# Modulation rows evacuated by ScalarE, chunk 0 turned behind two of the six modulation products, and the first loads in another order

## The reference

```python
mod = (_silu(L0_c) @ L0_wmod).reshape(L0_c.shape[0], 6, 1, -1)
sa, ca, ga, sb, cb, gb = (mod[:, 0], mod[:, 1], mod[:, 2], mod[:, 3], mod[:, 4], mod[:, 5])
ga = (2 * (ga >= 0) - 1) * jnp.maximum(jnp.abs(ga), 0.25)
gb = (2 * (gb >= 0) - 1) * jnp.maximum(jnp.abs(gb), 0.25)
h = _layernorm(x, axis=-1) * (1 + ca) + sa
x = x + ga * _L0_attn_ref(h, ...)   # 3 layers: linear attention with exp features, 16 heads; MLP 256-1024-256
h = _layernorm(x, axis=-1) * (1 + cb) + sb
x = x + gb * _L0_ffn_ref(h, ...)    # 2 layers: windowed softmax attention, 8 heads; gated MLP
```

## Time and profile before

| | |
|---|---|
| median of 3 runs | 2784.8 us (2779.9 to 2787.41) |
| profiled execution, its own time | 2785.39 us |
| its span, first to last instruction | 2783.6 us |
| TensorE busy | 2638.3 us (95%) |
| TensorE weight loads busy | 2145.3 us (77%) |
| VectorE busy | 2231.8 us (80%) |
| ScalarE busy | 1516.9 us (54%) |
| GpSimd busy | 1459.1 us (52%) |
| mean granted TensorE clock | 0.987 |

### The profile page before, as it was taken

The page is one execution under the profiler, slowest core; times in us unless marked ns, Lnnn a source line. Parts: engine busy times, 40 slices in busy tenths (PEclk is TensorE's granted clock), DMA queues, the critical chain, the costliest instruction groups (busy, mean ns, idle before and its releaser), DMA issues.

```text
span 2783.6 us, 61439 instructions
## 1 busy us (share of the span) xinstructions
PE 2638.3 (95%) x21416; PEld 2145.3 (77%) x21416; DVE 2231.8 (80%) x5244; ACT 1516.9 (54%) x3106; POOL 1459.1 (52%) x1408
## 2 busy tenths in 40 slices
PE   6799999999999999999888999999999999999986
PEld 4577787878788877778676788888878787888875
DVE  7678877787677777887998888888888888888874
ACT  3454455444544454445336766667666566676651
POOL 2343444443443345344476766665566666767643
PEclk9999999999999999999999999999999999999998
DMA  3100000010000000000111100000011100001001
GB/s 100 28 9 9 17 2 16 9 38 2 1 1 16 11 26 20 16 24 17 57 35 44 32 17 12 15 16 14 29 32 29 29 25 23 30 29 32 29 19 36
DMA packets 77715, 65.63 MB, mean 24 GB/s; under 512 B 15378, under 2 KB 72682, under 8 KB 77418
## 3 DMA queue, kind: packets, MB, share of 16 engines
q1 hardware_dynamic: 77418, 61.70, 7.5%
HBM read 49.10 MB, written 12.58 MB: 22 GB/s over the span
## 4 chain that ended last, share of the span: by engine, by line
PE 57%; DVE 21%; ACT 10%; issue 8%; POOL 2%; DMA 0%; DVEq 0%; SPq 0%; POOLq 0%; ACTq 0%
PE PS L273 49%; DVE U L1497 4%; PE PS L758 3%; DVE X L1370 2%; DVE ZC L1568 2%; ACT U L1007 2%; ACT U L1006 2%; ACT U L1008 2%; DVE ST L1351 2%; ACT U L1009 1%; DVE Z L1362 1%; ACT FB L1033 1%; PE PS L711 1%; PE PS L720 1%; DVE Z L1450 1%
## 5 line engine op out<-in xcount | busy, mean ns | idle before, releaser
L1188 ACT ACTIVATE PR<-PS,SM 128x256 f32<-128x256 f32 (+1 forms) x512 | 279.4, 555 | 102.3 <-DVE SM L1689 100.8
L1033 ACT ACTIVATE FB<-PS,BC 128x512 f32<-128x512 f32 x192 | 132.4, 689 | 293.1 <-PE PS L273 290.6
L2029 POOL TENSOR_TENSOR RL<-FB,RH 128x512 fp32r<-128x512 f32 x96 | 124.2, 1294 | 276.9 <-DVE RH L1475 276.9
L1497 DVE TENSOR_TENSOR U<-PS,CST 128x512 f32<-128x512 f32 x384 | 236.5, 678 | 24.7 <-PE PS L273 24.7
L1684 DVE CUSTOM_DVE_ANT_0 PS<-PS,MSK 128x256 f32<-128x256 f32 (+1 forms) x512 | 202.8, 436 | 48.1 <-PE PS L273 46.8
L1041 ACT COPY NUM<-PS 128x256 f32<-128x256 f32 x96 | 35.9, 373 | 354.9 <-DVE TMP L1489 303.7
L273 PE MATMUL PS<-W2H,RH 128*128 128x256 f32 x768 | 222.7, 290 | 4.5 <-DVE RL L1478 3.9
L1475 DVE CAST RH<-FB 128x512 fp32r<-128x512 f32 x192 | 87.8, 457 | 171.0 <-ACT FB L1033 167.4
L2154 POOL TENSOR_TENSOR SM<-SM,COL 128x8 f32<-128x8 f32 x128 | 215.1, 1680 | 10.7
L273 PE MATMUL PS<-W2H,RL 128*128 128x256 f32 x768 | 215.8, 281 | 0.0
L273 PE MATMUL PS<-W2L,RH 128*128 128x256 f32 x768 | 215.3, 280 | 0.0
(11 more groups left out here) (233 smaller groups left out, 9003.7 us busy)
## 6 DMA issues: line engine op xcount, KB each, us to landing
PX<-in_L_attn_x SPq DMA_DIRECT2D x16, 512.0 KB, 4.0
TB<-in_k_rot SPq DMA_DIRECT2D x64, 128.0 KB, 2.1
SG<-in_L_attn_W SPq DMA_DIRECT2D x24, 256.0 KB, 2.7
xp_scratch<-PX SPq DMA_DIRECT2D x8, 512.0 KB, 3.1
xs_scratch<-X SPq DMA_DIRECT2D x64, 64.0 KB, 1.5
ZS<-xs_scratch SPq DMA_DIRECT2D x16, 256.0 KB, 2.9
GG<-xp_scratch SPq DMA_DIRECT2D x8, 512.0 KB, 3.8
out<-GG SPq DMA_DIRECT2D x8, 512.0 KB, 3.7
```

Source lines behind the costliest of these rows:

```text
L1033: e.activation(FB[:, hb % 2, :], PS[:, 5, :], ACT.Relu, bias=BC[:, l % 2, 4 + hb:5 + hb]).then_inc(*a_re.up(n, hb))
L1188: t = e.activation(PR[:, par, 256 * i + lo:256 * i + hi], PS[:, 3 + par, 256 * i + lo:256 * i + hi], ACT.Exp, bias=S[:, 40 + 2 * g + i:41 ...
L1497: e.tensor_tensor(heads(U[:, u % 6, :], 4), heads(PS[:, g, :], 4), bcast(CM, 4), ALU.mult).then_inc(*d_mk.up(n, u))
L2029: e.tensor_tensor(RL[:, r, :], FB[:, 0, :], RH[:, r, :].bitcast(F), ALU.subtract).then_inc(*p_rl.up(n, hb))
```

## The change

In the head all six products are evacuated by ScalarE, the rows that need "1 +" with an activation whose bias is 1. TensorE makes products 0 and 1, turns chunk 0, and makes products 2 to 5, the last two in banks 5 and 6. VectorE goes from the first weight split straight to chunk 0. The constants' semaphore is split in three (`s_col`, `s_cst`, `s_hs`), so that each reader waits for its own. The loads are issued in another order. The first two rounds are written out call by call; waits that stood in the loops moved into the helpers, and some are now repeated.

```diff
-    MODS = [(0, 0, 4), (1, 0, 5), (0, 1, 6), (1, 1, 7), (0, 2, 0), (1, 2, 1)]
+    MODS = [(0, 0, 4), (1, 0, 5), (0, 1, 6), (1, 1, 7), (0, 2, 5), (1, 2, 6)]
@@ TensorE
-            if n == 0 and i < 2:
-                e.wait_ge(*a_mod.at(5))
+            if n > 0:
+                e.wait_ge(*d_am.at(n - 1, 1))
...
+        def modulate(i):
+            b, j, bank = MODS[i]
+            e.wait_ge(*d_cb.at(3))
+            if i < 2:
+                e.wait_ge(*s_wm0.at(1))
+            else:
+                e.wait_ge(*s_wm.at(1))
+            if i >= 4:
+                e.wait_ge(*a_mod.at(i - 3))
             for k in range(2):
                 t = mm(e, PS[:, bank, :], FB[:, 0, 128 * (2 * b + k):128 * (2 * b + k) + 128], FQ[:, k, j, :], k == 0)
             t.then_inc(*e_mod.up(i))
...
+        modulate(0)
+        modulate(1)
         turn_x(0)
+        modulate(2)
+        modulate(3)
+        modulate(4)
+        modulate(5)
+        proj(0, 0)
@@ ScalarE
+            if i == 0:
+                e.wait_ge(*s_col.at())
+            if j == 0:
+                e.activation(MOD[:, b, D:2 * D], PS[:, bank, 256:512], ACT.Identity, bias=ONE)
+                t = e.copy(MOD[:, b, 0:D], PS[:, bank, 0:256])
...
+        copy_modulation(0)
+        copy_modulation(1)
+        copy_modulation(2)
+        high_row(0, 0)
+        high_row(0, 1)
+        copy_modulation(3)
+        copy_modulation(4)
+        copy_modulation(5)
@@ VectorE
         prologue(0)
         split(0)
-        split(1)
-        e.wait_ge(*e_mod.at(0))
-        e.tensor_copy(modulation(0, 0), PS[:, MODS[0][2], :]).then_inc(*d_mod.up(0))
-        e.wait_ge(*d_mod.at(0))
-        e.tensor_scalar(MOD[:, 0, D:2 * D], MOD[:, 0, D:2 * D], 1.0, None, ALU.add, ALU.bypass).then_inc(*d_mod.up(1))
-        e.wait_ge(*d_mod.at(1))
         modulate_a(0)
         modulate_b(0)
+        split(1)
...
-        e.tensor_scalar(MOD[:, 1, D:2 * D], MOD[:, 1, D:2 * D], 1.0, None, ALU.add, ALU.bypass).then_inc(*d_mod.up(2))
-        e.tensor_scalar(MOD[:, :, 4 * D:5 * D], MOD[:, :, 4 * D:5 * D], 1.0, None, ALU.add, ALU.bypass).then_inc(*d_mod.up(3))
...
+        state(0, 2)
+        masks(0, 3)
+        prologue(2)
+        modulate_a(2)
+        lower(1, 0, 2, 0, a_x, d_x)
+        lower(1, 1, 3, 0, a_x, d_x)
+        state(0, 3)
+        modulate_b(2)
@@ GpSimd
+        key_state(0, 1)
+        rsqrt(("p", 2))
+        key_state(0, 2)
+        key_state(0, 3)
@@ SyncE
-        load_x(0)
+        e.dma_start(COL[:, :], ins["k_col"]).then_inc(*s_col.up())
         wm = ins["L0_wmod"].rearrange("(k p) n -> p k n", p=128)
         for k in range(2):
             e.dma_start(FQ[:, k, 0, :], wm[:, k, 0:512]).then_inc(*s_wm0.up(k))
-        e.dma_start(CST[:, :, :], ins["k_cst"]).then_inc(*s_cst.up(0))
-        e.dma_start(COL[:, :], ins["k_col"]).then_inc(*s_cst.up(1))
+        load_x(0)
+        e.dma_start(CST[:, :, :], ins["k_cst"]).then_inc(*s_cst.up())
         load_piece(0)
         load_piece(1)
+        load_columns(0)
         for k in range(2):
             e.dma_start(FQ[:, k, 1:3, :], wm[:, k, 512:1536].rearrange("p (j n) -> p j n", j=2)).then_inc(*s_wm.up(k))
```

More of the change, by code:

```diff
@@ L460, in scores @@
         def scores(n, j):
+            if j == 0:
+                for i in range(2):
+                    e.wait_ge(*a_kt.at(n, i))
+                    if n > 0:
+                        e.wait_ge(*d_z.at(n - 1, i))
+                    else:
+                        e.wait_ge(*a_fe.at(n, i))
             for m in range(2):
@@ L549, in _ @@
             t.then_inc(*e_mod.up(i))
-            if i == 1:
-                e.wait_ge(*s_cst.at(4))
+        modulate(0)
+        modulate(1)
         turn_x(0)
-        for n in range(24):
+        modulate(2)
[3 more added lines that the diff above has]
+        proj(0, 0)
+        proj(0, 1)
+        proj(0, 2)
+        proj(0, 3)
+        values(0, 0)
+        values(0, 1)
+        favor(0, 0, 2)
+        favor(0, 1, 3)
+        favor(0, 2, 0)
+        favor(0, 3, 1)
+        turn_k(0, 0)
+        turn_k(0, 1)
+        key_sums(0)
+        scores(0, 0)
+        sums(0, 0)
+        scores(0, 1)
+        sums(0, 1)
+        scores(0, 2)
+        sums(0, 2)
+        scores(0, 3)
+        turn_x(1)
+        sums(0, 3)
+        spread(0)
+        proj(1, 0)
+        proj(1, 1)
+        proj(1, 2)
+        proj(1, 3)
+        values(1, 0)
+        values(1, 1)
+        favor(1, 0, 2)
+        favor(1, 1, 3)
+        favor(1, 2, 0)
+        favor(1, 3, 1)
+        attn_out(0, 0)
+        attn_out(0, 1)
+        turn_k(1, 0)
+        turn_k(1, 1)
+        key_sums(1)
+        scores(1, 0)
+        sums(1, 0)
+        scores(1, 1)
+        sums(1, 1)
+        scores(1, 2)
+        sums(1, 2)
+        scores(1, 3)
+        turn_h(0)
+        turn_x(2)
+        sums(1, 3)
+        for n in range(2, 24):
             live, w, m = n < 24, n - 1, n - 2
@@ L1054, in _ @@
             else:
-                e.copy(modulation(b, j), PS[:, bank, 0:256])
+                e.activation(MOD[:, b, 1024:1280], PS[:, bank, 0:256], ACT.Identity, bias=ONE)
                 t = e.copy(GB[:, b, :], PS[:, bank, 256:512])
             t.then_inc(*a_mod.up(i))
[L1058 to L1061, removed]
+        exponent()
+        copy_modulation(0)
+        copy_modulation(1)
+        copy_modulation(2)
@@ new lines, in _ @@
+        numerators(0, 3)
+        operands(1, 0)
+        operands(1, 1)
+        operands(1, 2)
+        operands(1, 3)
+        attention(0, 0)
+        attention(0, 1)
+        features(1, 0, 2)
+        features(1, 1, 3)
+        features(1, 2, 0)
+        features(1, 3, 1)
+        keep_rows(1, 0)
+        keep_rows(1, 1)
+        numerators(1, 0)
+        numerators(1, 1)
+        numerators(1, 2)
+        high_mid(0, 0)
+        high_mid(0, 1)
+        high_row(2, 0)
+        high_row(2, 1)
@@ L1525, in _ @@
         modulate_b(1)
[L1526 to L1529 removed]
+        add_bv(0, 0)
+        add_bv(0, 1)
+        split(3)
+        running(0, 0)
+        running(0, 1)
+        carry(0)
+        gate_steps(0)
+        gate_steps(1)
+        normaliser(0)
+        masks(0, 0)
+        split(4)
+        state(0, 0)
+        masks(0, 1)
+        split(5)
+        state(0, 1)
+        masks(0, 2)
+        split(6)
+        state(0, 2)
[6 more added lines that the diff above has]
+        modulate_b(2)
+        scale_num(0, 0)
+        scale_num(0, 1)
+        split(7)
+        split(8)
+        add_bv(1, 0)
+        add_bv(1, 1)
+        split(9)
+        running(1, 0)
+        running(1, 1)
+        carry(1)
+        add_wo(0)
+        norm1_a(0)
+        normaliser(1)
+        masks(1, 0)
+        split(10)
+        norm1_b(0)
+        state(1, 0)
+        masks(1, 1)
+        split(11)
+        state(1, 1)
+        masks(1, 2)
+        state(1, 2)
+        masks(1, 3)
+        prologue(3)
+        modulate_a(3)
+        lower(0, 0, 0, 1, a_h, d_h)
+        lower(0, 1, 1, 1, a_h, d_h)
+        lower(2, 0, 2, 0, a_x, d_x)
+        lower(2, 1, 3, 0, a_x, d_x)
+        state(1, 3)
+        modulate_b(3)
+        for n in range(2, 24):
             live, w, m, z = n < 24, n - 1, n - 2, n - 3
```

282 lines of the change are left out of this document (169 added, 113 removed).

## The result

| | before | after |
|---|---|---|
| median of 5 runs | 2785.09 us (2779.9 to 2787.41) | 2794.94 us (2790.03 to 2795.91) |
| profiled execution: time, span | 2785.39, 2783.6 us | 2793.17, 2791.3 us |
| mean granted TensorE clock | 0.987 | 0.983 |

The ratio of the runs is 1.0030, 95% interval 1.0019 to 1.0042: about 8.4 us slower (the two medians lie 9.9 us apart). That is small, but the interval leaves out 1. The profiled executions differ by 7.7 us of span; 7.3 had been predicted.

What follows compares the result with a forecast made beforehand. The prediction took the chain through the first projection's start and the ends of rounds 0 and 1 to set the time; 3.0 + 1.0 + 3.3 = +7.3 us gave 2792.7 profiled, 2792.1 against the median, range 2783 to 2798.

Steps and rivals of the forecast that it cites:

- rival A: Head and ends of rounds 0 and 1: both moves cost, clock falls once or twice; +3 to +11 us, chance 0.62.
- Second weights: Head, SyncE's queue: second modulation weights issued between 10.5 and 12.7 us, landing at 16.7, bounds 15.1 and 18.3.
- Head, size: Start of the first projection: +0.5 us from late weights and +2.5 from the clock, +3.0 in all (-0.7 to +5.5).
- Chunk 0 in time, and waiting: Head: chunk 0 ready at 14.5 us, turned by 15.5, before the second weights land; brought forward by 5 us.
- End of round 0: Last sums on TensorE wait for GpSimd's key-state sum behind its rsqrt; +1.0 us, 0 to +2.0.
- a slow projection: Behind the end of round 0: the next projection may run slow, up to 1 us more.
- End of round 1: Statistics moved behind the masks delay rsqrt and sums: +2.3 us, plus half of 2.0 for the clock; +3.3 (2.3 to 4.3).
- The sum: Whole kernel: head 3.0, end of round 0 1.0 and end of round 1 3.3 make +7.3 us.
- rival C: Round 0's first sums: clock holds, up to half of 10.2 us comes back; -1.9 us, 2782.9, chance 0.08.
- No drift back: From round 2 on: time won or lost by its start stays to the end; later rounds giving it back would be wrong.

Runs made afterwards that it cites:

- the changed GpSimd order: The changed kernel with GpSimd's rsqrt of chunks 2 and 3 moved behind the key-state sum of tile 2; 2789.2 us, 1.0008 of the kernel before.
- the order alone: The kernel before with only VectorE's order in rounds 0 and 1 changed as in the change; 2790.88 us, 1.0016 of the kernel before.
- the throwaway products: The changed kernel with two unused TensorE products behind product 1 and two behind the turn of chunk 0; 2790.01 us, 1.0014 of the kernel before.
- turn last: Changed kernel with columns behind second weights, chunk 1 before row loads, VectorE's old order, and chunk 0's turn behind all six products; 2787.52 us, 1.0006.
- the head without the stall repeated: Changed kernel with columns behind second weights, chunk 1 before row loads, VectorE's old order; run again on a second chip: 2786.48 us, 1.0002.
- the head alone: The changed kernel with VectorE's old order put back in rounds 0 and 1; 2789.07 us, 1.0011 of the kernel before.
- round 0 swapped repeated: Changed kernel, columns behind second weights, chunk 1 before row loads, old order in round 1, round 0's key-state sum before rsqrt; third chip: 2781.32 us, 0.9983.

## Why the prediction was right

Slower by 7.3 us was forecast and about 8 came, by rival A's mechanism: late weights, a fallen clock, and last sums that wait for GpSimd. That both moves cost is shown by the experiments; that the sum came so close is partly luck. By its steps:

- **Second weights.** The stall came whole: 2.62 us for the first omega, issue at 12.89 (12.6 was the upper bound, and 12.7 the latest that would have shown the forecast right), landing at 17.94 (16.7 taken, 15.1 to 18.3). The middle value was too low for this execution, but not out of reach: in three others with the same loads in front the weights were issued at 11.78, 12.49 and 13.58 and landed at 16.70, 17.54 and 18.58, the last a little beyond the upper bound. The Trainium skill (page "DMA: Bandwidth & Descriptors", section "Rules for kernel authors") says that a non-contiguous last dimension lowers to one descriptor per element; that the stall would come whole was the prediction's own step from it. The trace went to that side, and omegas without columns ahead of them issued at 0.46 us each.
- **Head, size.** +3.27 at the projection against +3.0, by other shares: the late weights cost 1.9 (18.07 + 6.84 - 23.02) where 0.5 stood, the clock 1.4 (8.22 us from product 2 to the projection, for 6.84) where 2.5 stood.
- **Chunk 0 in time, and waiting.** Ready at 14.56 (14.5 taken), turned by 16.59, predicted 15.5; the turn was at the low clock. Against the kernel before it was ready 3.5 us earlier (18.08 there) and turned some 5 us earlier. Products 0 and 1 ended at 12.48; the "near 12" of the prediction doesn't fit its own landing at 6.1 with eight passes of 0.85, which gives 12.9.
- **End of round 0.** Masks to numerators +1.62 against +1.0, inside 0 to 2.0, with 0.85 more for a slow projection, as bounded. Released by SBD behind the rsqrt, as said; the changed GpSimd order shows it.
- **End of round 1.** +3.64 against +3.3. With the clock up, the order alone gives +2.36 (2.3 predicted); with it down, the change gives +3.64 (4.3 predicted).
- **The sum** held partly by luck. The head's loss did not stay whole: of +3.59 only +0.86 was left at the masks of tile 1. Of the 2.7 us given back, 1.7 is the part of rival C that was given 0.08: round 0's first sums had stood at half clock for 10.2 us, and now for 6.8. The other 0.9 no rival had: a running sum on VectorE that no longer ran beside a weight split on GpSimd. Against it, round 0 cost 0.6 more than in the sum, the slow projection behind it 0.85 (0.8 of which was given back in round 1), and from round 2 on another 1.5 us were added. There TensorE's time at half clock is larger (61.8 us against 55.3; in all 95.9 against 75.7), and half of the difference would be enough, but no run separates this.
- **How long the cold stretch at round 0's first sums is** does not follow from the head alone. With the throwaway products it was 6.8 us and another 3.4 before it; with the operands at 24.6, 25.1, 25.4 and 26.1 (turn last, the head without the stall repeated, the head alone, round 0 swapped repeated) it was 3.4, 3.4, 6.8 and 3.4.
- **No drift back.** What rounds 0 and 1 hand on stays: +6.2 at the numerators of round 1 is +7.3 at the last running sum, and nothing is given back.

## What to carry to other kernels

Before an instruction is moved ahead of a block on one engine, look at what the other engines have in their own order behind that block: here the masks came early, but GpSimd's rsqrt stood ahead of the sum that TensorE needed, and one swap of two lines turned +1.6 us into -2.0 at the numerators of round 0. Then look again further on: 0.7 of the 2.0 were left at the next operands, and in round 1 the same swap only uncovered VectorE as the next bound. A load that stalls the queue delays whatever is put behind it, so moving it helps only when nothing urgent follows. With the same loads in front the operands of round 0 started between 25.4 and 29.2 us in three executions, so a gain of 0.1% must be seen on more than one chip before it is believed.

## What was not expected of the hardware

- The issue of the eight small omega loads took 3.70 to 3.78 us in the head with no column load ahead of them. Right behind the three column loads it took 5.02 to 6.04 in four executions, and 5.88 to 6.69 in eight others that had the 1 MB of weights ahead as well. For the next layer, behind the same three column loads but with few other loads on the way, it took 3.81 to 3.83 in twelve of the fourteen traces, 4.48 and 4.99 in the other two.
- Behind product 1 TensorE paused for 1.4 to 3.4 us, and the length of the pause does not tell whether the clock was at half over the turn behind it. With pauses of 1.36, 1.69, 2.09, 2.69 and 3.40 us the turn took 1.09 to 1.10; with 2.03, 2.14 (three times) and 2.59 it took 1.78 to 1.97. One and the same kernel was on either side in its two profiled executions (1.36 and 2.03).
- A clock held up at one place was partly paid for at the next: 2.07 us won by throwaway products in the head were 0.8 us at round 0's masks.
- The same running sum on VectorE took 2.26 us where it started beside a weight split on GpSimd (before), and 1.23 with GpSimd idle (after).
